# Softmax loop of a one-layer vision tower: class sums and class exponentials taken for two pairs at once

## The chip, the core and the metric

One core of a Trainium2 chip. The metric is the device time of one execution in microseconds, the median of three runs. The profile is of one further execution, with every instruction's start and duration.

## The reference

32 images of 128x128 become 64 patches each. A noisy gated embedding (two linear layers, Mish, product, a third linear layer) gives 64 tokens of 128 features per image, to which the position code is added; a class token is put in front, so an image has 65 tokens. Then one attention layer with 8 heads of 16 features and relative positions in keys and values, and a mixture of 8 experts with the two best per token. What matters here is the attention:

```
attn = softmax((q k^T + q relk[j - i]) / sqrt(128))      # 65 x 65 per image and head
out  = attn v + sum_j attn[i, j] relv[j - i]
h    = h + out Wo + bo
```

All data are float32.

## The kernel before, in words

The program is written engine by engine: each engine has its own list of instructions in a fixed order, and the engines meet only at semaphores. The change lies in the attention's softmax loop. It works on **pairs of images**, 16 of them, numbered p (PAIRS = 16). In the loop the 64 patch queries of two images lie on the 128 partitions after a transpose; the 64 patch keys of 8 heads are 512 columns. The class key's score and the class query's probabilities are kept apart, as 8 columns a pair and one row an image.

Ahead of the loop, eight A2 steps of TensorE make the relative key scores; ScalarE (line 517) and VectorE (line 794) copy each step out of PSUM. From step 4 on TensorE also transposes, after each step, one block of the class key products (turn_cls, line 1224), which VectorE sums (red, line 789).

Iteration p of VectorE's loop, in order (softmax, then the calls behind it), with the short names used below:
- **sum** (line 820): adds the class exponential of pair p-2 to that pair's sum of exponentials; waits for ScalarE.
- **max** (824): over the transposed scores of pair p, in PSUM; waits for TensorE's turn_scores(p) (line 1276).
- **bias** (832): minus the scaled max, or the class score where larger (top and nSc, both in SBUF). ScalarE's exponentials of pair p wait for it.
- **reciprocal** (838) of pair p-2's sum. GpSimd waits for it.
- **class product** (914, odd p from 5): the class key's own share in the output; reads PSUM and vcq.
- **score add** (808): scores of pair p+1 from PSUM plus A2 from SBUF. turn_scores(p+1) waits for it.
- **probability copy** (849, probs(p-3)): the transposed probabilities of pair p-3 from PSUM to PT; waits for TensorE's turn_probs(p-3) (line 1298).
- p = 2: class_scores (859 to 863); p = 3: class_probs (867 to 873), the class query's probabilities p0d and p0x; p = 4: class_turned (883, 884), which puts their transposes into column 64 of PT.
- **value copy** (900) and **class copy** (902), odd p from 7: four images' attended values from PSUM to OT, and their class column to OTc.

ScalarE computes, for each pair, 8 exponentials with row sums (541, one per head) and one of the class column (544). GpSimd, in iteration p: **difference** (374), the class exponent of pair p; **normalisation** (384) of pair p-2's 512 columns by the reciprocal; **class share** (385); in odd iterations **repeat** (392). TensorE, in iteration p: turn_scores(p), scores(p+1), in iteration 4 the transposes of p0d (1344), from p = 15 fillers (keep_warm) and turn_pc, then turn_probs(p-3), which waits for the normalisation of pair p-3 (semaphore pn_ok), then from p = 5 values(p-5); values(0) also waits for class_turned (ptc_ok). The slots of exponentials, SP, are four; bias, sum and reciprocal (ntop, esum, rsum) have two slots.

Behind the loop TensorE runs the relative values, in between with fillers, the output projection and the experts.

## Time and profile before

| | us |
|---|---|
| median of 3 runs | 261.53 (260.9 to 262.17) |
| the profiled execution | 261.36 |
| its span, first to last instruction | 259.5 |
| TensorE busy, matmuls | 236.2 (91%) |
| VectorE busy | 153.7 (59%) |
| ScalarE busy | 132.5 (51%) |
| GpSimd busy | 64.4 (25%) |
| chain of waits, by engine | PE 63%, DVE 17%, issue 6%, ACT 4%, POOL 4%, DMA 4% |

The names in the profile: PE is TensorE's matmul, PEld its weight load, DVE VectorE, ACT ScalarE, POOL GpSimd, SP the engine that issues most transfers. The softmax loop is from about 72 to 118 us of the span. A row's duration includes the end of the engine's pipeline, so a following instruction that waits for nothing starts up to 0.1 us before the row ends; distances from start to start are what add up.

### The profile page before, as it was taken

Reading aid. Unit: us, or ns where it says so; the run is one execution under the profiler, and the core shown is the slowest. Engines: PE = TensorE matmul, PEld = TensorE weight load, DVE = VectorE, ACT = ScalarE, POOL = GpSimd, SP = SyncE. Lnnn points to the kernel's source line nnn. Section 1 sums busy time; section 2 is a strip of 40 time slices with the busy share of each in tenths; the row PEclk is TensorE's granted clock in tenths of the full one; section 3 lists DMA queues with packets and bytes.
Section 4 is the critical chain, followed back from the end, with each engine's and each line's share of the span. In section 5 each row is a group of like instructions: output and inputs, shape, how many; then the busy total and the mean of one; then the engine's idle time right before and its main releaser. Section 6 shows DMA issues by size and latency. Waiting matters only on the chain.

```text
span 259.5 us, 6469 instructions
## 1 busy us (share of the span) xinstructions
PE 236.2 (91%) x2507; PEld 202.2 (78%) x2507; DVE 153.7 (59%) x485; ACT 132.5 (51%) x442; POOL 64.4 (25%) x104
## 2 busy tenths in 40 slices
PE   0989999899886788899999999999999999999994
PEld 0755656599754566677878999799999999999993
DVE  0496798844479999996367749625060605152463
ACT  1543137872179899994047894451708080807100
POOL 8930112087015556667132300000000000000000
PEclk9999999999999999999999999999999999999999
DMA  6970000000003407054000000000000000000015
GB/s 210 287 177 3 0 1 0 0 4 3 3 0 68 98 15 150 4 172 158 5 3 3 0 3 0 4 0 3 1 0 3 0 0 3 0 3 0 1 30 137
DMA packets 10938, 10.05 MB, mean 39 GB/s; under 512 B 1121, under 2 KB 9679, under 8 KB 10780
## 3 DMA queue, kind: packets, MB, share of 16 engines
q1 hardware_dynamic: 8412, 7.88, 11.2%
q10 hardware_dynamic: 1952, 1.41, 1.9%
q8 instruction: 20, 0.33, 0.5%
q0 software_dynamic: 544, 0.35, 0.5%
q14 instruction: 10, 0.08, 0.1%
HBM read 7.52 MB, written 2.11 MB: 37 GB/s over the span
## 4 chain that ended last, share of the span: by engine, by line
PE 63%; DVE 17%; issue 6%; ACT 4%; POOL 4%; DMA 4%; ACTq 1%; DVEq 0%; POOLq 0%
PE banks L1075 58%; DMA region_d<-in_L_tok_W_sw 4%; DVE top L824 4%; DVE stb L808 3%; POOL w_lo L405 2%; ACT region_e L541 2%; PE banks L1276 2%; POOL rstd L338 2%; DVE stb L728 2%; DVE region_c L849 2%; DVE stats L710 1%; DVE h L701 1%; PE banks L1396 1%; ACT w_hi L549 1%; PE banks L1085 1%
## 5 line engine op out<-in xcount | busy, mean ns | idle before, releaser
L1065 DVE SCALAR_TENSOR_TENSOR KT<-banks,vbd,KT 128x128 f32<-128x128 f32 (+1 forms) x136 | 38.0, 342 | 54.3 <-PE banks L1075 53.8
L563 ACT ACTIVATE region_d<-banks,vecs 128x416 f32<-128x416 f32 x80 | 45.5, 610 | 44.5 <-PE banks L1075 44.4
L1075 PE MATMUL banks<-w_all,region_d 128*128 128x128 f32 (+1 forms) x544 | 63.0, 275 | 0.0
L1075 PEld LDWEIGHTS banks<-w_all,region_d 128*128 128x128 f32 (+1 forms) x544 | 61.4, 187 | 1.2 <-ACT region_d L563 0.2
L541 ACT ACTIVATE region_e<-banks,ntop 128x64 f32<-128x64 f32 x128 | 38.7, 362 | 6.5 <-DVE ntop L832 3.5
L541 ACT ACTIVATION_READ_ACCUMULATOR region_e<-banks,ntop 128x1 f32 x128 | 31.8, 255 | 0.0
L1075 PE MATMUL banks<-x_hi,w_hi 128*128 128x416 f32 x80 | 29.9, 373 | 0.0
L1075 PE MATMUL banks<-x_lo,w_hi 128*128 128x416 f32 x80 | 28.2, 353 | 0.0
L1075 PE MATMUL banks<-x_hi,w_lo 128*128 128x416 f32 x80 | 28.2, 352 | 0.0
L1276 PE MATMUL banks<-kc,stb 128*128 128x128 f32 x64 | 10.5, 286 | 8.1 <-DVE stb L808 8.0
L1075 PEld LDWEIGHTS banks<-x_hi,w_hi 128*128 128x128 f32 x80 | 15.1, 188 | 2.4 <-issue 1.2
L384 POOL TENSOR_TENSOR region_e<-region_e,rsum 128x512 f32<-128x512 f32 (+1 forms) x16 | 16.3, 1017 | 0.3 <-PE banks L1323 0.2
L1075 PE MATMUL banks<-kc 128*128 128x128 f32 x56 | 10.3, 314 | 6.5 <-DMA kc<-in_consts 6.5
L1075 PE MATMUL banks<-region_d,relk_bd 64*128 64x64 f32 x256 | 15.3, 288 | 0.0
L1075 PEld LDWEIGHTS banks<-x_lo,w_hi 128*128 128x128 f32 x80 | 15.0, 188 | 0.2
L1075 PEld LDWEIGHTS banks<-x_hi,w_lo 128*128 128x128 f32 x80 | 15.0, 188 | 0.2
L1276 PEld LDWEIGHTS banks<-kc,stb 128*128 128x128 f32 x64 | 6.7, 140 | 10.8 <-DVE stb L808 10.8
L1075 PEld LDWEIGHTS banks<-region_d,relk_bd 64*128 64x128 f32 x256 | 14.6, 188 | 0.6 <-issue 0.5
L1075 PE MATMUL banks<-region_b,wnT 128*128 128x512 f32 x32 | 14.8, 599 | 0.0
L1075 PEld LDWEIGHTS banks<-kc 128*128 128x128 f32 x56 | 8.0, 208 | 7.4 <-DMA kc<-in_consts 6.5
L824 DVE TENSOR_REDUCE top<-banks 128x8 f32<-128x512 f32 x16 | 11.0, 687 | 1.9 <-PE banks L1276 1.4
L1075 PE MATMUL banks<-region_d,region_b 64*128 64x128 f32 x128 | 11.4, 297 | 0.3 <-ACT region_a L517 0.3
(217 smaller groups left out, 367.8 us busy)
## 6 DMA issues: line engine op xcount, KB each, us to landing
region_a<-in_x SPq DMA_DIRECT2D x2, 512.0 KB, 6.3
region_a<-in_x SPq DMA_DIRECT2D x1, 1024.0 KB, 10.7
out<-h SPq DMA_DIRECT2D x2, 512.0 KB, 5.6
h<-out SPq DMA_DIRECT2D x4, 256.0 KB, 4.5
w_sb<-in_L_ffn_W SPq DMA_DIRECT2D x1, 1024.0 KB, 5.6
region_d<-in_L_attn_rel_v SPq DMA_DIRECT2D x2, 260.0 KB, 10.0
out<-KT SPq DMA_DIRECT2D x6, 64.0 KB, 1.8
out<-KT ACTq DMA_DIRECT2D x6, 64.0 KB, 2.0
```

What stands on the lines that cost most here:

```text
L338: g.tensor_tensor(rstd[:, n * TPB:(n + 1) * TPB], ve[:, n * TPB:(n + 1) * TPB], mhalf[:, :], ALU.pow).then_inc(S["rstd_ok"], 1)
L384: g.tensor_tensor(ev, ev, rv, ALU.mult).then_inc(S["pn_ok"], 1)
L405: g.tensor_tensor(w1_lo[:, :], w1_sb[:, :], w1_hi[:, :].bitcast(F32), ALU.subtract).then_inc(S["w1_split"], 1)
L541: last = a.activation(dst[:, h // 2, h % 2], src[:, h // 2, h % 2], ACT.Exp, scale=SCALE, bias=ntop[:, o + h:o + h + 1], accum_out=esum[:, ...
L563: a.activation(HB[:, e % 2, s, blk * FB:(blk + 1) * FB], bank[h_bank(i)][:, 0:FB], ACT.Gelu, bias=vecs[:, v:v + 1]).then_inc(S["gelu_ok"], 1)
L728: last = v.tensor_scalar(ST[n % 2][0:m, i * C:(i + 1) * C], src[0:m, t * C:(t + 1) * C], mv[0:m, 2 * t:2 * t + 1], rstd[0:m, t:t + 1], ALU ...
L808: v.tensor_tensor(ST[p % 2].rearrange("p (g j m) -> p g j m", g=2, j=2), banks[:, 0:1024].rearrange("p (g h j m) -> p g h j m", g=2, h=2, ...
L824: most = mark(v.tensor_reduce(top[:, o].rearrange("p (j s) -> p j s", j=PJ), bank[2 + p % 2][:, :].rearrange("p (j k s) -> p j s k", j=PJ, ...
L849: v.tensor_copy(PT[:, :, 2 * p:2 * p + 2, 0:NPATCH], bank[4 + p % 2][:, :].rearrange("p (j b q) -> p j b q", j=PJ, b=2)).then_inc(S["pt_ok ...
L1065: last = v.scalar_tensor_tensor(acc[0:m, t, :], bank[out_bank(u)][0:m, i * C:(i + 1) * C], comb[0:m, t, e:e + 1], acc[0:m, t, :], op0=ALU. ...
L1075: return t_.matmul(o, l, r, start=start, stop=stop)
L1276: last = t_.transpose(bank[2 + p % 2][:, j * P:(j + 1) * P], ST[p % 2][:, j * P:(j + 1) * P], ident)
```

## The change

- The sums of exponentials, the reciprocals, the differences, the class exponentials and the class shares are computed once for two pairs (in odd iterations; pairs 14 and 15 each by themselves). ntop, esum and rsum get four slots. In VectorE's odd iterations sum and reciprocal stand first, ahead of the max; GpSimd then does the class share of both pairs, the normalisation of pair p-3, the difference, the normalisation of pair p-2.
- The class query's probabilities (p0x, p0d) are made by GpSimd in its iteration 3. Their transposes follow turn_probs(1) in TensorE's iteration 4; class_turned stands in VectorE's iteration 5 and is two copies of one half of the partitions each.
- The value copy takes the class column along (260 columns); OTc becomes a part of OT. A column of zeros in tmpx is set once.
- The A2 steps use other banks; the fourth turn_cls stands behind scores(0), which waits for seven evictions instead of eight.

```diff
+        SPc = region_e[:, :].rearrange("p (n c) -> p n c", n=4)[:, :, 512:520]
+        xnT = sb("xnT", ALL)
         OT = xnT
         OTq = OT[:, :].rearrange("p (q b) -> p q b", b=IMG)
-        OTc = sb("OTc", IMG)
+        OTc = OT[:, TOK:ALL]
...
-        ntop = sb("ntop", 2 * H)
-        esum = sb("esum", 2 * H)
-        rsum = sb("rsum", 2 * H)
+        ntop = sb("ntop", 4 * H)
+        esum = sb("esum", 4 * H)
+        rsum = sb("rsum", 4 * H)
...
-            return (2 if i % 2 == 0 else 0) + g
+            return (2, 4, 0, 2, 0, 2, 0, 2)[i] + g
+
+        def group(p):
+
+            return p // 2 if p < PAIRS - 2 else p - 7
+
+        def closes(p):
+
+            return p % 2 == 1 or p >= PAIRS - 2
+
+        def members(p):
+
+            n = 2 if p < PAIRS - 2 else 1
+            first = (p - n + 1) % 4
+            return n, slice(first, first + n), slice(H * first, H * (first + n))
...
             def difference(p):
 
-                o = slice(8 * (p % 2), 8 * (p % 2) + 8)
+                n, slots, cols = members(p)
                 pool.wait_ge(S["top_ok"], p + 1)
                 if p >= 4:
-                    pool.wait_ge(S["pc_ok"], p - 3)
-                g.tensor_tensor(SP[p % 4][:, 512:520], ntop[:, o], nSc[:, p * H:(p + 1) * H], ALU.subtract)\
+                    pool.wait_ge(S["pc_ok"], group(p - 4) + 1)
+                g.tensor_tensor(SPc[:, slots], ntop[:, cols].rearrange("p (n h) -> p n h", h=H),
+                                nSc[:, (p - n + 1) * H:(p + 1) * H].rearrange("p (n h) -> p n h", h=H), ALU.subtract)\
                     .then_inc(S["dc_ok"], 1)
 
+            def class_share(p):
+
+                n, slots, cols = members(p)
+                pool.wait_ge(S["r_ok"], group(p) + 1)
+                g.tensor_tensor(PcA[:, (p - n + 1) * H:(p + 1) * H].rearrange("p (n h) -> p n h", h=H), SPc[:, slots],
+                                rsum[:, cols].rearrange("p (n h) -> p n h", h=H), ALU.mult).then_inc(S["pc_ok"], 1)
+
             def normalised(p):
 
-                pool.wait_ge(S["r_ok"], p + 1)
-                e_, r_ = SP[p % 4], rsum[:, 8 * (p % 2):8 * (p % 2) + 8]
+                e_, r_ = SP[p % 4], rsum[:, H * (p % 4):H * (p % 4) + H]
                 js = PJ if p < PAIRS - 1 else PJ // 2
                 ev = e_[:, 0:P * js].rearrange("p (j s k) -> p j s k", j=js, s=2)
                 rv = r_[:, 0:2 * js].rearrange("p (j s) -> p j s", j=js).unsqueeze(3).to_broadcast([P, js, 2, NPATCH])
                 g.tensor_tensor(ev, ev, rv, ALU.mult).then_inc(S["pn_ok"], 1)
-                g.tensor_tensor(PcA[:, p * H:(p + 1) * H], e_[:, 512:520], r_, ALU.mult).then_inc(S["pc_ok"], 1)
 
             def repeat(u):
 
-                pool.wait_ge(S["pc_ok"], 2 * u + 2)
+                pool.wait_ge(S["pc_ok"], group(2 * u + 1) + 1)
                 if u >= 2:
                     pool.wait_ge(S["pcT_ps"], u - 1)
                 g.tensor_copy(pc_rep[:, 2 * (u % 2):2 * (u % 2) + 2, :, :].rearrange("p r h d -> p (r h) d"),
                               PcA[:, 16 * u:16 * u + 16].unsqueeze(2).to_broadcast([P, 16, HD]))\
                     .then_inc(S["rep_ok"], 1)
 
+            def class_probs():
+
+                pool.wait_ge(S["cr_ok"], 1)
+                link(g.tensor_tensor(sml[:, 10:12], cv[:, :, NPATCH], sml[:, 8:10], ALU.mult))
+                g.tensor_tensor(p0x[:, :].rearrange("p (r b) -> p r b", b=2),
+                                kc[:, K_PR:K_PR + PAIRS].unsqueeze(2).to_broadcast([P, PAIRS, 2]),
+                                sml[:, 10:12].unsqueeze(1).to_broadcast([P, PAIRS, 2]), ALU.mult)
+                g.tensor_tensor(p0d[:, :].rearrange("p (b s k) -> p b s k", b=2, s=2),
+                                cv[:, :, 0:NPATCH].unsqueeze(2).to_broadcast([P, 2, 2, NPATCH]),
+                                sml[:, 8:10].unsqueeze(2).unsqueeze(3).to_broadcast([P, 2, 2, NPATCH]), ALU.mult)\
+                    .then_inc(S["p0d_ok"], 1)
+
             for p in range(PAIRS + 2):
-                if p < PAIRS:
+                r = p - 2
+                if r >= 0 and closes(r):
+                    class_share(r)
+                    normalised(r - 1 if r < PAIRS - 2 else r)
+                if p < PAIRS and closes(p):
                     difference(p)
-                if p >= 2:
-                    normalised(p - 2)
-                    if p % 2 == 1:
-                        repeat((p - 3) // 2)
+                if 0 <= r < PAIRS - 2 and closes(r):
+                    normalised(r)
+                if p >= 3 and p % 2 == 1:
+                    repeat((p - 3) // 2)
+                if p == 3:
+                    class_probs()
...
                 act.wait_ge(S["top_ok"], p + 1)
                 if p >= 4:
                     act.wait_ge(S["pt_ps"], p - 3)
-                    act.wait_ge(S["pc_ok"], p - 3)
-                if p >= 2:
-                    act.wait_ge(S["r_ok"], p - 1)
-                o = 8 * (p % 2)
+                    act.wait_ge(S["r_ok"], group(p - 4) + 1)
+                o = H * (p % 4)
                 src = bank[2 + p % 2][:, :].rearrange("p (j k s) -> p j s k", j=PJ, s=2)
                 dst = SP[p % 4][:, 0:512].rearrange("p (j s k) -> p j s k", j=PJ, s=2)
                 for h in range(H):
                     last = a.activation(dst[:, h // 2, h % 2], src[:, h // 2, h % 2], ACT.Exp, scale=SCALE,
                                         bias=ntop[:, o + h:o + h + 1], accum_out=esum[:, o + h:o + h + 1])
-                act.wait_ge(S["dc_ok"], p + 1)
-                last = a.activation(SP[p % 4][:, 512:520], SP[p % 4][:, 512:520], ACT.Exp)
                 last.then_inc(S["e_ok"], 1)
+                if closes(p):
+                    n, slots, cols = members(p)
+                    act.wait_ge(S["dc_ok"], group(p) + 1)
+                    a.activation(SPc[:, slots], SPc[:, slots], ACT.Exp).then_inc(S["ec_ok"], 1)
...
-                if r is not None:
-                    q = slice(8 * (r % 2), 8 * (r % 2) + 8)
-                    dve.wait_ge(S["e_ok"], r + 1)
-                    total = mark(v.tensor_tensor(esum[:, q], esum[:, q], SP[r % 4][:, 512:520], ALU.add))
+                if r is not None and closes(r):
+                    n, slots, cols = members(r)
+                    dve.wait_ge(S["ec_ok"], group(r) + 1)
+                    if r >= 4:
+                        dve.wait_ge(S["pn_ok"], r - 3)
+                        dve.wait_ge(S["pc_ok"], group(r - 4) + 1)
+                    total = v.tensor_tensor(esum[:, cols].rearrange("p (n h) -> p n h", h=H),
+                                            esum[:, cols].rearrange("p (n h) -> p n h", h=H), SPc[:, slots], ALU.add)
+                    after(mark(total))
+                    v.reciprocal(rsum[:, cols], esum[:, cols]).then_inc(S["r_ok"], 1)
                 if p is not None:
-                    o = slice(8 * (p % 2), 8 * (p % 2) + 8)
+                    o = slice(H * (p % 2), H * (p % 2) + H)
+                    o4 = slice(H * (p % 4), H * (p % 4) + H)
                     dve.wait_ge(S["s_ps"], p + 1)
                     most = mark(v.tensor_reduce(top[:, o].rearrange("p (j s) -> p j s", j=PJ),
                                                 bank[2 + p % 2][:, :].rearrange("p (j k s) -> p j s k", j=PJ, s=2),
                                                 axis=AX_X, op=ALU.max))
-                if p is not None:
                     after(most)
-                    if p >= 2:
-                        dve.wait_ge(S["e_ok"], p - 1)
-                        dve.wait_ge(S["dc_ok"], p - 1)
-                    v.scalar_tensor_tensor(ntop[:, o], top[:, o], -SCALE, nSc[:, p * H:(p + 1) * H], op0=ALU.mult,
+                    if p >= 4:
+                        dve.wait_ge(S["e_ok"], p - 3)
+                        dve.wait_ge(S["dc_ok"], group(p - 4) + 1)
+                    v.scalar_tensor_tensor(ntop[:, o4], top[:, o], -SCALE, nSc[:, p * H:(p + 1) * H], op0=ALU.mult,
                                            op1=ALU.min).then_inc(S["top_ok"], 1)
-                if r is not None:
-                    after(total)
-                    if r >= 2:
-                        dve.wait_ge(S["pc_ok"], r - 1)
-                    v.reciprocal(rsum[:, q], esum[:, q]).then_inc(S["r_ok"], 1)
...
                 link(v.tensor_reduce(r2, cv, axis=AX_X, op=ALU.add))
-                link(v.reciprocal(sml[:, 8:10], r2))
-                v.tensor_tensor(p0d[:, :].rearrange("p (b s k) -> p b s k", b=2, s=2),
-                                cv[:, :, 0:NPATCH].unsqueeze(2).to_broadcast([P, 2, 2, NPATCH]),
-                                sml[:, 8:10].unsqueeze(2).unsqueeze(3).to_broadcast([P, 2, 2, NPATCH]), ALU.mult)
-                link(v.tensor_tensor(sml[:, 10:12], cv[:, :, NPATCH], sml[:, 8:10], ALU.mult))
-                v.tensor_tensor(p0x[:, :].rearrange("p (r b) -> p r b", b=2),
-                                kc[:, K_PR:K_PR + PAIRS].unsqueeze(2).to_broadcast([P, PAIRS, 2]),
-                                sml[:, 10:12].unsqueeze(1).to_broadcast([P, PAIRS, 2]), ALU.mult)\
-                    .then_inc(S["p0d_ok"], 1)
+                v.reciprocal(sml[:, 8:10], r2).then_inc(S["cr_ok"], 1)
 
             def class_turned():
                 dve.wait_ge(S["p0T_ps"], 1)
-                for b2 in range(2):
-                    pv = bank[6][:, b2 * P:(b2 + 1) * P].rearrange("p (r j s) -> p r j s", r=PAIRS, j=PJ)
-                    tv = ptt[:, :].rearrange("p (r j) -> p r j", j=PJ)
-                    link(v.tensor_scalar(tv, pv[:, :, :, 1], kc[:, K_KP + 1:K_KP + 2], None, ALU.mult))
-                    last = v.scalar_tensor_tensor(PT[:, :, b2:IMG:2, NPATCH].rearrange("p j r -> p r j"),
-                                                  pv[:, :, :, 0], kc[:, K_KP:K_KP + 1], tv, op0=ALU.mult,
-                                                  op1=ALU.add)
-                    if b2 == 0:
-                        link(last)
+                for s in range(2):
+                    hs = slice(NPATCH * s, NPATCH * (s + 1))
+                    last = v.tensor_copy(PT[hs, :, :, NPATCH].rearrange("p j (r b) -> p j r b", b=2),
+                                         bank[6][hs, 0:256].rearrange("p (b r j s) -> p j r b s", b=2, r=PAIRS, j=PJ)
+                                         [:, :, :, :, s])
                 last.then_inc(S["ptc_ok"], 1)
...
-                v.scalar_tensor_tensor(OTq[:, :, 4 * u:4 * u + 4].rearrange("p q b -> p b q"), o[:, :, 0:NPATCH],
-                                       vecs[:, V_BV:V_BV + 1], own(u), op0=ALU.add, op1=ALU.add)
-                v.tensor_copy(OTc[:, 4 * u:4 * u + 4], o[:, :, NPATCH]).then_inc(S["w1_ev"], 1)
+                v.scalar_tensor_tensor(OT[:, :].rearrange("p (q b) -> p q b", b=IMG)[:, :, 4 * u:4 * u + 4]
+                                       .rearrange("p q b -> p b q"), o,
+                                       vecs[:, V_BV:V_BV + 1], own(u), op0=ALU.add, op1=ALU.add).then_inc(S["w1_ev"], 1)
...
-                if p == 4:
+                if p == 5:
...
-                if i >= 4:
+                if 4 <= i < 7:
                     turn_cls(i - 4)
 
             def scores(p):
                 if p == 0:
-                    pe.wait_ge(S["a2_evA"], 8)
-                    pe.wait_ge(S["a2_evD"], 8)
+                    pe.wait_ge(S["a2_evA"], 7)
+                    pe.wait_ge(S["a2_evD"], 7)
...
+            turn_cls(3)
             for p in range(PAIRS + 5):
                 if p < PAIRS:
                     turn_scores(p)
...
-                if p == 4:
-                    pe.wait_ge(S["p0d_ok"], 1)
-                    for b2 in range(2):
-                        last = t_.transpose(bank[6][:, b2 * P:(b2 + 1) * P], p0d[:, b2 * P:(b2 + 1) * P], ident)
-                    last.then_inc(S["p0T_ps"], 1)
...
                     turn_probs(p - 3)
+                if p == 4:
+                    pe.wait_ge(S["p0d_ok"], 1)
+                    for b2 in range(2):
+                        last = t_.transpose(bank[6][:, b2 * P:(b2 + 1) * P], p0d[:, b2 * P:(b2 + 1) * P], ident)
+                    last.then_inc(S["p0T_ps"], 1)
                 if p >= 5:
                     values(p - 5)
```

## Rows read from the trace of the kernel before

**Rows 1.** Windows view, one steady period: length, then busy us and count by engine.

```profile
94.11:99.53 5.42, 4.72 (x70) 3.48 (x68) 5.28 (x17) 5.07 (x37) 3.13 (x7) 1.00 0.53 115
```

**Rows 2.** Timeline, VectorE, one period: start us, duration us, engine, line, operation.

```profile
94.18 0.68 DVE L824 TENSOR_REDUCE top<-banks 128x8 f32<-128x512 f32 x1
94.89 0.17 DVE L832 SCALAR_TENSOR_TENSOR ntop<-top,nSc 128x8 f32<-128x8 f32 x1
...
95.09 0.67 DVE L808 TENSOR_TENSOR stb<-banks,region_a 128x512 f32<-128x512 f32 x1
95.68 0.68 DVE L849 COPY region_c<-banks 128x512 f32<-128x512 f32 x1
96.28 0.15 DVE L820 TENSOR_TENSOR esum<-esum,region_e 128x8 f32<-128x8 f32 x1
96.51 0.69 DVE L824 TENSOR_REDUCE top<-banks 128x8 f32<-128x512 f32 x1
...
97.44 0.42 DVE L914 TENSOR_TENSOR tmpx<-banks,vcq 128x256 f32<-128x256 f32 x1
97.79 0.68 DVE L808 TENSOR_TENSOR stb<-banks,region_a 128x512 f32<-128x512 f32 x1
...
98.98 0.65 DVE L900 SCALAR_TENSOR_TENSOR xnT<-banks,vecs,tmpx 128x256 f32<-128x256 f32 x1
99.48 0.16 DVE L902 COPY OTc<-banks 128x4 f32<-128x4 f32 x1
```

**Rows 3.** Timeline, GpSimd and TensorE in the same period.

```profile
95.14 0.20 POOL L374 TENSOR_TENSOR region_e<-ntop,nSc 128x8 f32<-128x8 f32 x1 [1.23 <-DVE ntop L832]
95.30 1.04 POOL L384 TENSOR_TENSOR region_e<-region_e,rsum 128x512 f32<-128x512 f32 x1
...
95.82 0.66 PE L1276 MATMUL banks<-kc,stb 128*128 128x128 f32 x4 [0.47 <-DVE stb L808]
```

**Rows 4.** Timeline, VectorE: a sum and its reciprocal with nothing between.

```profile
115.20 0.15 DVE L820 TENSOR_TENSOR esum<-esum,region_e 128x8 f32<-128x8 f32 x1
115.39 0.20 DVE L838 RECIPROCAL rsum<-esum 128x8 f32<-128x8 f32 x1
```

**Rows 5.** Timeline: VectorE instructions beside GpSimd ones, at two places.

```profile
77.67 1.05 POOL L384 TENSOR_TENSOR region_e<-region_e,rsum 128x512 f32<-128x512 f32 x1
...
78.39 0.34 DVE L861 TENSOR_SCALAR sml<-sml 128x2 f32<-128x2 f32 x1
...
88.31 0.40 POOL L392 COPY region_d<-PcA 128x256 f32<-128x256 f32 x1
...
88.53 0.20 DVE L820 TENSOR_TENSOR esum<-esum,region_e 128x8 f32<-128x8 f32 x1
```

**Rows 6.** Timeline, VectorE: from the last A2 eviction to the first probability copy.

```profile
68.92 0.69 DVE L794 COPY region_a<-banks 128x512 f32<-128x512 f32 x1 [1.27 <-PE banks L1075]
...
70.47 0.69 DVE L808 TENSOR_TENSOR stb<-banks,region_a 128x512 f32<-128x512 f32 x1 [0.85 <-PE banks L1075]
...
79.10 0.16 DVE L820 TENSOR_TENSOR esum<-esum,region_e 128x8 f32<-128x8 f32 x1
...
80.65 0.68 DVE L849 COPY region_c<-banks 128x512 f32<-128x512 f32 x1
```

**Rows 7.** Timeline: class scores, first values, max of pair 6, half normalisation.

```profile
78.77 0.29 DVE L862 TENSOR_TENSOR cx<-banks,sml 128x128 f32<-128x128 f32 x1
...
86.22 0.44 PE L1075 MATMUL banks<-region_c,vbd 128*32 128x65 f32 x16
...
88.77 0.69 DVE L824 TENSOR_REDUCE top<-banks 128x8 f32<-128x512 f32 x1
...
117.15 0.61 POOL L384 TENSOR_TENSOR region_e<-region_e,rsum 128x256 f32<-128x256 f32 x1 [0.25 <-PE banks L1323]
```

**Rows 8.** Timeline, TensorE: transposed probabilities of pairs 12 and 13.

```profile
112.83 0.60 PE L1298 MATMUL banks<-kc,region_e 128*128 128x128 f32 x4
...
115.03 0.66 PE L1298 MATMUL banks<-kc,region_e 128*128 128x128 f32 x4
```

More of the change, by code:

```diff
@@ L913, in class_key @@
                     dve.wait_ge(S["w1_ev"], u - 1)
-                v.tensor_tensor(own(u), bank[u % 2][:, 256:512].rearrange("p (b q) -> p b q", q=NPATCH),
+                v.tensor_tensor(own(u)[:, :, 0:NPATCH], bank[u % 2][:, 256:512].rearrange("p (b q) -> p b q", q=NPATCH),
                                 vcq[:, :].unsqueeze(1).to_broadcast([P, 4, NPATCH]), ALU.mult)\
@@ L949, in attended_class @@
                 dve.wait_ge(S["w2_ps"], 5)
-                link(v.scalar_tensor_tensor(OTc[:, :], bank[4][:, 0:IMG], vecs[:, V_BV:V_BV + 1], OTc[:, :],
-                                            op0=ALU.add, op1=ALU.add))
-                v.scalar_tensor_tensor(OTc[:, :], bank[4][:, IMG:2 * IMG], clsv[:, 5:6], OTc[:, :], op0=ALU.mult,
+                link(v.tensor_tensor(OTc, bank[4][:, 0:IMG], OTc, ALU.add))
+                v.scalar_tensor_tensor(OTc, bank[4][:, IMG:2 * IMG], clsv[:, 5:6], OTc, op0=ALU.mult,
                                        op1=ALU.add).then_inc(S["oc_ok"], 1)
@@ L1441, in _ @@
             pe.wait_ge(S["oc_ok"], 1)
-            mm(bank[6][0:IMG, 0:C], OTc[:, :], wo).then_inc(S["opc_ps"], 1)
+            mm(bank[6][0:IMG, 0:C], OTc, wo).then_inc(S["opc_ps"], 1)
             pe.wait_ge(S["w1_split"], 1)
```

17 lines of the change are left out of this document (8 added, 9 removed).

## The prediction

> **What bounds the kernel now.** I read the page first: its engine table and slices say that TensorE is busy nearly everywhere and always at the full granted clock (1.0, the 2.4 GHz level), except in the slices of the softmax loop, 72 to 118 us, where VectorE shows nines and TensorE fives to nines. The chain of waits says the same: inside the loop it runs over VectorE's instructions, with a short hop to TensorE for each transpose. Behind the loop it is TensorE again, without a gap worth naming, so a shift of the loop's end moves the end of the kernel by the same amount. Then the windows: in one steady period of two pairs VectorE is busy 5.28 of 5.42 us, ScalarE 5.07, TensorE 4.72, GpSimd 3.13 [rows 1]. VectorE's own issue order is the bound; ScalarE is close behind. The loop is a fixed order of waits, so I read one period instruction by instruction [rows 2] and worked out the same period, and then the start and the tail, with the new order.
>
> I count from an odd iteration's class sum. Start to start on VectorE [rows 2]: max to bias 0.71; bias over reciprocal to score add 0.20 (I split it 0.09 and 0.11); score add to probability copy 0.59; probability copy to whatever follows 0.60; class product to score add 0.35; value copy to class copy 0.50 and 0.05 from there to the next sum, at 99.53, the window's edge [rows 1]; sum to max 0.07. A max cannot start before its transposes are done: 0.69 from their start at 95.82 to 96.51 [rows 2, 3].
>
> **The period, part by part.** *Removed from VectorE:* in even iterations the sum (0.07) and the reciprocal (0.11); the class copy (0.05), for which the value copy grows from 256 to 260 columns (+0.01, estimated from its 0.50). In odd iterations sum and reciprocal stay, but the reciprocal now stands before the max and waits for the sum: 0.19 [rows 4], then 0.11 to the max. Before, the max waited for TensorE anyway (sum at 96.28, max at 96.51), so the max moves from 0.23 to 0.30. The bias follows at 1.01, the class product at 1.10, the score add at 1.45 and the probability copy could start at 2.04. Had nothing else to be waited for, the period would be 2.04 + 0.60 + 0.51 + 0.71 + 0.09 + 0.59 + 0.60 = 5.14, or 0.29 less than now.
>
> *ScalarE:* half of the class exponentials go, and its wait for the reciprocal becomes one for the bias alone. It is 0.35 short of the period already [rows 1], so this is worth nothing while VectorE sets the pace, and it would be needed only below about 5 us.
>
> *The new wait, GpSimd to TensorE to VectorE.* The reciprocal of pairs p-3 and p-2 now comes in iteration p, and the same iteration copies out the transposed probabilities of pair p-3. Before, pair p-3 was normalised one iteration earlier. So in each odd iteration: reciprocal at 0.19, its 0.20 and 0.08 to GpSimd (bias at 94.89 with 0.17, GpSimd at 95.14) [rows 2, 3] gives 0.47; the class share in front costs 0.16 to the next instruction [rows 3] and I take 0.18 for its 16 columns; the normalisation runs from 0.65 to 1.69 (1.04 [rows 3]); TensorE starts 0.06 later (the score add ends at 95.76, transposes 95.82) at 1.75; the copy can start at 2.44. That is 0.40 after the 2.04. By itself this makes the period 5.54, already 0.11 longer than now. Behind the waiting copy on VectorE stand the value copy and the even max; on TensorE the values and the next transposes stand behind the waiting transposes, but end before VectorE wants them (1.75 + 1.0 + 0.69 = 3.44 against 3.70).
>
> *Two engines on one port.* Now the normalisation (0.65 to 1.69) lies across the odd bias (1.01), which reads two SBUF tensors, top and nSc. Today it never does: the normalisation always starts after the bias. What happens when they meet is seen at two places [rows 5]. The scalar operation on two columns at 78.39 takes 0.34 and ends at 78.73, and the normalisation beside it ends at 78.72. The sum at 88.53 takes 0.20 where rows 2 and 4 have 0.15, and ends at 88.73, with the GpSimd copy beside it ending at 88.71. Instructions that read PSUM and one SBUF tensor, the score add and the probability copy from 95.09 on, run through a normalisation unchanged (0.67, 0.68) [rows 2, 3]. So I let the bias end at 1.69 + 0.02 = 1.71 instead of 1.18; the class product then starts at 1.65 (0.08 before that end, as all followers do), the score add at 2.00, the probability copy at 2.59, which is later than its 2.44, the value copy at 3.19, even max 3.70, bias 4.41, score add 4.50, probability copy 5.09, next sum 5.69. **Period 5.69, +0.26.** The bound below for this hold is 0 (then 5.54); the bound above is the normalisation's whole 1.04 on the bias (+0.4 more), and I take the value by the row at 78.39.
>
> The Trainium skill (SBUF — State Buffer, section "Who interferes with whom") states this as a rule: a VectorE instruction with two SBUF inputs contends with a GpSimd instruction that reads SBUF, and whoever comes first holds the shared ports for its whole instruction. The two rows agree with it.
>
> **Start of the loop.** Scores of pair 0 no longer stand behind the fourth class transpose nor behind the last eviction. They are over by about 69.6, and the score add starts when the last eviction ends, 68.92 + 0.69 = 69.61, so at 69.65 instead of 70.47 [rows 6]: -0.82. The bank change in the eight A2 steps: TensorE had no gap there, so 0. Iteration 2 loses a reciprocal (-0.11). The sum of iteration 3 moves from 79.10 [rows 6] to 78.17. But iteration 3 is the first odd one: its probability copy comes at 78.17 + 2.44 = 80.61, against 80.65 now [rows 6]. The 0.93 us are gone.
>
> **Class query.** In iteration 3 a reduction and a reciprocal remain (0.6 + 0.42 with the copy before them, estimated from instructions of their size), so max 4 starts at 81.63. GpSimd gets its operands at 81.80, does two small ones (0.27 and 0.20, as in rows 3 with one wait) and the 256 columns in 0.61 (the half normalisation of rows 7), until 82.88. Bias 4 wants to start at 82.34 and reads two SBUF tensors: held to 82.90. Score add 82.84, copy 83.43, sum 5 at 84.03. Iteration 5 has the period's waits: copy at 86.62. Then the class column, two copies of 128 columns at 0.29 [rows 7], 87.22 to 87.83. Moved here, they now gate the values of pair 0, which stand before the next score transposes in TensorE's order: 87.89, 0.40 for the 16 matmuls (the row at 86.22 has 0.44 with the pipeline's end), 0.69 for the transposes: **max 6 at 88.98, against 88.77 [rows 7]: +0.21.** All of the shorter class code is spent in this wait. The bounds: 0.9 earlier, if the values did not stand in the way, or 0.3 later, if the 64-row copies take as long as they would for twice the columns.
>
> **To the end of the loop.** Sum 7 comes 0.71 + 0.09 + 0.59 + 0.60 = 1.99 later, at 90.97, sum 9 at 96.66 (now 96.28), +0.38; three more periods at +0.26 give sum 15 at 113.74, +1.16. In iteration 15 no score add is left to fill VectorE, and the last ones behind it are set by TensorE: transposes of pair 12 now start at 112.83 [rows 8], then at 113.74 + 1.75 = 115.49: +2.66. Values, ten filler matmuls and the transposes of pair 13 follow 2.20 later as now (115.03 [rows 8]); in today's kernel those fillers covered a wait, now they lie on the path. One class copy less on VectorE gives back 0.06. **Sum: -0.82 - 0.11 + 1.14 (to max 6) + 0.17 + 0.78 + 1.50 - 0.06 = +2.60.** The profiled execution took 261.36 us for a span of 259.5, against the median of 261.53; 261.36 + 2.60 = 263.96 and 261.53 + 2.60 = 264.13, so I say 264.0.
>
> **Rivals.** *A, both waits as argued: 264.0, chance 0.45,* its own range 263.2 to 265.2. *B, the bias is not held:* only the GpSimd to TensorE wait remains. Iteration 4 gives 0.39 back, iteration 5 0.15, the four later periods 0.60: +1.46, 262.8. For it: the held rows are a scalar operation and a sum, none is a bias. 0.17. *C, faster:* normalisation ends before VectorE needs the copy, so the released instructions count in full: -0.93 at the start, six periods at -0.29 (-1.74), class parts about -1.0 (five small instructions less): 257.7. It decides from where the way from sum to copy takes less than 2.04 instead of 2.44; against it, every link of the 2.44 is a row. With ScalarE bounding, or half of the waits, it is 259 to 260. 0.12. *D, no change:* the waits are each some 0.2 shorter and the tail's 1.5 is partly absorbed, which leaves 260.5 to 262.5. For it: GpSimd spans are rough. 0.16. *E, more contention:* the class product, whose vcq is in SBUF, and the copies are held too, 0.2 a period and more in the tail: 265.8. 0.10.
>
> **Numbers.** A change under 0.5% (1.3 us) cannot be told from none here. Range 261.0 to 266.0: it leaves out most of C and the lower edge of D. Slower is A, E and half of B, with a little of D: 0.66; same is the rest of B and D: 0.23; faster 0.11.
>
> **What would show it.** Right: in odd iterations of the profile after, the bias takes some 0.6 to 0.7 us instead of 0.17 and ends with the normalisation; the period is 5.7; max 6 is preceded by a wait for TensorE behind values 0; in the tail the transposes of pair 12 wait for GpSimd and start 2.7 later. Wrong, if the period is under 5.43, or the bias keeps its 0.17 (B), or the probability copies of odd iterations follow the score add at once (C).

## The result, and the profile after

| | before | after |
|---|---|---|
| median, us | 261.55 (260.90 to 262.17, 4 runs) | 266.05 (265.40 to 268.82, 4 runs) |
| profiled execution, us | 261.36 | 266.37 |
| its span, us | 259.5 | 264.6 |
| mean granted clock of TensorE | 1.0 | 0.993 (the other three runs: 0.979, 0.992, 0.992) |

The ratio is 1.0192 (95%: 1.0116 to 1.0269): slower by 4.5 us, where 2.6 was predicted. The median lies 0.05 us above the predicted range. Ratios, here and below, leave out executions that took over 1.5% longer than the fastest of the same kernel.

The page of the kernel after: engine totals, then the slices of TensorE, VectorE, GpSimd and TensorE's granted clock.

```profile
PE 238.9 (90%) x2507; PEld 205.1 (78%) x2507; DVE 154.9 (59%) x459; ACT 132.1 (50%) x435; POOL 63.2 (24%) x93
...
PE   0999999899976698779999999999999999999993
...
DVE  0485798844579789998176838636060515152553
...
POOL 8930112187006345557312300000000000000000
PEclk9999999999999899999999999999999999999999
```

TensorE is busy 2.7 us longer with the same 2507 matmuls, and one slice of its clock is an 8, where the page of before has nines throughout. The steady periods and the stretch in front of them, by windows (columns as in [rows 1]; the clock is the third from the end):

```profile
104.61:110.32 5.71, 4.73 (x68) 3.48 (x67) 5.61 (x14) 5.05 (x35) 2.79 (x5) 1.00 0.02 3
...
90.00:92.00 2.00, 2.00 (x15) 1.48 (x13) 1.55 (x3) 0.77 (x5) 0.00 (x0) 0.61 0.03 8
92.00:94.00 2.00, 2.00 (x24) 1.55 (x22) 1.08 (x4) 1.70 (x12) 0.55 (x2) 0.54 0.02 8
```

The period is 5.71 us against 5.42 [rows 1]. TensorE and ScalarE do in it what they did before; VectorE has three instructions fewer (14 against 17), and yet is busy 0.33 longer. Its timeline shows why (start, duration):

```profile
104.61 0.17 DVE L862 TENSOR_TENSOR esum<-esum,region_e 128x16 f32<-128x16 f32 x1
104.81 0.25 DVE L865 RECIPROCAL rsum<-esum 128x16 f32<-128x16 f32 x1
104.97 0.63 DVE L870 TENSOR_REDUCE top<-banks 128x8 f32<-128x512 f32 x1
105.64 0.74 DVE L877 SCALAR_TENSOR_TENSOR ntop<-top,nSc 128x8 f32<-128x8 f32 x1
106.31 0.41 DVE L942 TENSOR_TENSOR tmpx<-banks,vcq 128x256 f32<-128x256 f32 x1
106.64 0.67 DVE L847 TENSOR_TENSOR stb<-banks,region_a 128x512 f32<-128x512 f32 x1
107.24 0.68 DVE L889 COPY region_c<-banks 128x512 f32<-128x512 f32 x1
```

and GpSimd's and TensorE's beside it (in brackets the idle time before a row, and what ended it):

```profile
105.14 0.22 POOL L397 TENSOR_TENSOR PcA<-region_e,rsum 128x16 f32<-128x16 f32 x1 [2.83 <-DVE rsum L865]
105.32 1.04 POOL L406 TENSOR_TENSOR region_e<-region_e,rsum 128x512 f32<-128x512 f32 x1
```

```profile
106.42 0.66 PE L1325 MATMUL banks<-kc,region_e 128*128 128x128 f32 x4 [0.75 <-POOL region_e L406]
```

The odd bias takes 0.74 instead of 0.17 and ends at 106.38; the normalisation beside it ends at 106.36. TensorE's transposes wait 0.75 for the same normalisation. Both predicted waits stand in these ten rows.

Ahead of the periods, TensorE in iterations 5 and 6:

```profile
89.24 0.44 PE L1102 MATMUL banks<-region_c,vbd 128*32 128x65 f32 x16 [1.68 <-DVE region_c L913]
89.61 0.66 PE L1303 MATMUL banks<-kc,stb 128*128 128x128 f32 x4
90.20 1.03 PE L1102 MATMUL banks<-region_d,region_b 64*128 64x128 f32 x8
91.16 1.11 PE L1325 MATMUL banks<-kc,region_e 128*128 128x128 f32 x4
```

The values of pair 0 have waited 1.68 us for class_turned. Right behind it four transposes take 1.11 instead of 0.66, while the windows show the granted clock at 0.61 and 0.54: for 3.4 us the clock was on the 1.2 GHz level (0.5 of the full one). The kernel before idles too, 1.42 us in its longest wait here, and keeps its clock:

```profile
88.07 0.66 PE L1276 MATMUL banks<-kc,stb 128*128 128x128 f32 x4 [1.42 <-DVE stb L808]
```

The waits of the kernel after in 72 to 124 us (total, times, longest):

```profile
PE banks L1325 <- POOL region_e L406: 5.7, 6, 1.4
DVE top L870 <- PE banks L1303: 3.3, 4, 1.2
```

The milestones, each as a difference of start times on VectorE or TensorE, put the whole beside the forecast. "Clock held" is a kernel of the experiments (fill_all).

| stretch | before | forecast | after | clock held |
|---|---|---|---|---|
| last A2 eviction to max 6 | 19.85 | +0.21 | +0.52 | +0.53 |
| max 6 to sum 9 | 7.51 | +0.17 | +1.08 | +0.22 |
| sum 9 to sum 15 (three periods) | 16.30 | +0.78 | +0.84 | +0.83 |
| sum 15 to the first relative value | 7.55 | +1.44 | +1.29 | +1.31 |
| sum | 51.21 | +2.60 | +3.73 | +2.89 |

The span grew by 5.1: 3.73 here, 0.36 behind the loop, and 1.01 before it. The eight A2 steps, whose banks are changed, have no part in the 1.01: from the first of their evictions on VectorE to the last it is 14.81 before and 14.82 after. In front of them the change alters no instruction. The last eviction started anywhere from 68.4 to 70.0 in the profiles of all kernels, and at 69.93, 69.28 and 68.73 in the three of the changed one, so the 1.01 is scatter of one profile.

### The profile page after: what moved, and what is told of

It is laid out like the page before. It is cut to its first block, busy times and chain, and to the rows that moved or that the text cites. A ratio compares the mean times of both kernels' runs of the same rounds, so it can differ in the third digit from the quotient of the medians.

```text
span 264.6 us, 6397 instructions
## 1 busy us (share of the span) xinstructions
PE 238.9 (90%) x2507; PEld 205.1 (78%) x2507; DVE 154.9 (59%) x459; ACT 132.1 (50%) x435; POOL 63.2 (24%) x93
## 4 chain that ended last, share of the span: by engine, by line
PE 63%; DVE 18%; issue 7%; POOL 4%; ACT 3%; DMA 3%; SPq 1%; DVEq 0%; POOLq 0%
PE banks L1102 58%; DVE top L870 3%; DVE region_c L889 3%; DMA rows<-in_L_tok_W_sb 3%; DVE stb L847 2%; POOL w_lo L444 2%; POOL rstd L353 2%; DVE stb L767 2%; PE banks L1112 1%; DVE stats L749 1%; PE banks L1303 1%; ACT region_e L578 1%; DVE h L740 1%; PE banks L1424 1%; ACT w_hi L588 1%
## 5 line engine op out<-in xcount | busy, mean ns | idle before, releaser
L578 ACT ACTIVATION_READ_ACCUMULATOR region_e<-banks,ntop 128x1 f32 x128 | 28.7, 226 | 0.0
L1102 PE MATMUL banks<-kc 128*128 128x128 f32 x56 | 11.4, 341 | 6.5 <-DMA kc<-in_consts 6.5
L1325 PE MATMUL banks<-kc,region_e 128*128 128x128 f32 x64 | 10.8, 293 | 5.8 <-POOL region_e L406 5.7
L1102 PEld LDWEIGHTS banks<-kc 128*128 128x128 f32 x56 | 9.1, 234 | 7.4 <-DMA kc<-in_consts 6.5
L1325 PEld LDWEIGHTS banks<-kc,region_e 128*128 128x128 f32 x64 | 7.1, 145 | 8.1 <-POOL region_e L406 6.9
```

The source lines that it names most:

```text
L578: last = a.activation(dst[:, h // 2, h % 2], src[:, h // 2, h % 2], ACT.Exp, scale=SCALE, bias=ntop[:, o + h:o + h + 1], accum_out=esum[:, ...
L1102: return t_.matmul(o, l, r, start=start, stop=stop)
L1325: last = t_.transpose(bank[4 + p % 2][:, j * P:(j + 1) * P], SP[p % 4][:, j * P:(j + 1) * P], ident)
```

## Experiments

All experiments run beside the kernel before, whose medians were 262.02, 262.02, 261.35 and 261.61 in the four groups. My theory was the prediction's: two waits, the clock a third cause that it had left out. The rivals: the class query's order, contention elsewhere, or the clock as the whole loss.

**1. One half of the change at a time.** pair_only is the kernel before with sums, reciprocals, differences and class exponentials of two pairs. rest_early is the opposite: no pairing, everything else of the change, with class_turned in iteration 4.

```
rest_early: sum, reciprocal, difference, normalisation, class share per pair, as before
            GpSimd makes p0x, p0d; class column in the value copy; scores(0) early
-                if p == 5:      # class_turned
+                if p == 4:
```

> The kernel before with the pairing alone: sums, reciprocals, differences, class exponentials and class shares for two pairs. No other start of the loop, class query on VectorE as before, class column copied by itself. Theory of the two waits (late normalisation, bias held beside it): period of two pairs 5.71 plus 0.05 for the class copy against 5.43, in the tail the transposes of pair 12 another 1.5 later: together +3.0 to +4.0, 264.5 to 265.5. Rival (the pairing is harmless, the class parts and the clock make the loss): 261 to 262.

> The changed kernel without the pairing (sums, reciprocals and exponentials pair by pair as before), with the early start of the loop, GpSimd's class probabilities and the class column in the value copy, and class_turned in iteration 4. Theory: no late normalisation and no held bias, so the gains count: 0.7 at the start, 0.5 to 0.7 for the class query, 0.05 a period for the class copy: 259.5 to 260.3. Rival (the other edits gain nothing because another engine sets the pace): 261.5.

Measured: pair_only 266.59, over its forecast of 264.5 to 265.5, ratio 1.0176 (1.0149 to 1.0203), period 5.77; its clock fell once, behind a wait of 1.95 us in front of the transposes. rest_early 259.14, under its forecast of 259.5 to 260.3, ratio 0.9893 (0.9874 to 0.9911): faster than both kernels by more than the interval. Its period:

```profile
92.01:97.38 5.37, 4.72 (x72) 3.48 (x70) 5.22 (x15) 5.05 (x37) 3.13 (x7) 1.00 0.52 111
```

The pairing alone costs 4.6 us, as much as the whole change; the rest alone gains 2.9. From the last A2 eviction to the first relative value pair_only takes 4.95 longer than before and rest_early 1.86 less; the other 1 us of rest_early's gain in the times stands in no stretch of the loop.

rest_late is rest_early with class_turned back in iteration 5, as the change has it:

```
-                if p == 4:
+                if p == 5:
```

> As e6_rest_early, but with class_turned in iteration 5, as the change has it. Theory: the first values wait behind it on TensorE and max 6 comes 0.5 to 1.2 us later than with class_turned in iteration 4: 259.7 to 260.3 beside 259.1, and the clock may fall once. Rival: nothing, 259.1.

Measured: 261.21 (10 runs), ratio 0.9983 (0.9946 to 1.0019), no change. Max 6 comes 0.94 later behind the last eviction than in rest_early, and TensorE shows why:

```profile
88.17 0.44 PE L1091 MATMUL banks<-region_c,vbd 128*32 128x65 f32 x16 [1.97 <-DVE region_c L902]
```

So moving class_turned costs about 1 us on the path. In the times it costs more, and the forecast of 259.7 to 260.3 missed: rest_late is 0.4 under the kernel before beside it, rest_early 2.9. Part of this goes with the clock: rest_late's five executions at a mean clock of 0.997 or more took 260.7 on average, the five at 0.993 or less 262.0. In this profile the clock held in spite of 1.97 us of idle time: the idle place makes the fall possible, not certain.

The two halves as the change has them, +4.6 and −0.4, come near its 4.5. What rest_early gains is not kept beside the pairing: rest_early has its first probability copy 0.71 sooner behind the last eviction than the kernel before, the changed kernel 0.06 later, because there the copy waits for the normalisation.

**2. The class query's wait in the changed kernel.** early_turn sets class_turned back to iteration 4; fill keeps it in 5 and gives TensorE six filler matmuls in front of the values of pair 0.

```
early_turn:
-                if p == 5:      # VectorE, class_turned
+                if p == 4:
fill:
+                if p == 5:
+                    keep_warm(6, spare=7)
```

> The changed kernel with class_turned in VectorE's iteration 4 instead of 5; its input is there (transposes end at 84.46, VectorE arrives at 85.11). Theory: TensorE's wait of 1.7 us for the class column goes and with it the fall of the clock; max 6 comes about 1.2 us earlier and the stretch behind it 0.9 shorter, so about 263.9. Rival: the two copies (0.77 us) delay sum 5, normalisation and all behind it by as much as they save, 265.5 or more.

> The changed kernel with six filler matmuls on TensorE ahead of the first values, where TensorE stands idle for 1.7 us behind the class column (89.24). The wait itself stays. Theory K (the clock): the granted clock does not fall to 0.5 behind this idle time, so the stretch from max 6 to sum 9 shrinks from 8.59 us to about 7.7, and the kernel gains 0.9 us, about 265.1. Rival W (only the waits count, the clock costs nothing on the path): nothing, 266.0. If the fillers outlast the wait, up to 0.2 is lost.

Measured: early_turn 265.46, ratio 1.0135 (1.0116 to 1.0154); fill 266.03, ratio 1.0152 (1.0134 to 1.0171). In early_turn the wait for class_turned is gone and max 6 comes 0.91 sooner behind the last eviction, but the clock fell all the same, in the transposes behind the wait for the normalisation:

```profile
87.52 0.66 PE L1325 MATMUL banks<-kc,region_e 128*128 128x128 f32 x4 [1.57 <-POOL region_e L406]
...
90.06 1.11 PE L1325 MATMUL banks<-kc,region_e 128*128 128x128 f32 x4
```

In fill the clock held where the fillers were (max 6 to max 8 took 5.75, against 6.60 after; the forecast had 5.69), but fell earlier, in an idle place that they did not cover:

```profile
80.00:82.00 2.00, 0.92 (x6) 0.72 (x7) 1.68 (x4) 1.73 (x13) 1.90 (x4) 0.86 0.00 0
82.00:84.00 2.00, 2.00 (x13) 1.44 (x12) 1.93 (x5) 1.66 (x12) 1.51 (x5) 0.50 0.39 89
```

Neither forecast held in the time: there is more than one place for the fall. fill's 266.03 is what the rival (the clock costs nothing) had. Its two executions at a mean clock of 0.998 and 1.0 took 265.96 and 266.11, the two at 0.994 and 0.992 took 266.82 and 265.61: in these times no gain of a held clock can be seen.

**3. The pairing's two waits, one at a time.** recip_behind puts the double reciprocal behind the bias, so that the bias cannot be held and the normalisation comes later. share_behind lets GpSimd do the first normalisation before the class share.

```
share_behind:
+                    pool.wait_ge(S["r_ok"], group(r) + 1)
-                    class_share(r)
                     normalised(r - 1 if r < PAIRS - 2 else r)
+                    class_share(r)
```

> The changed kernel with the reciprocal of two pairs behind the bias again, as in the kernel before. The normalisation of GpSimd then starts after the bias. Theory of the held port: the odd bias is back at 0.17 us (0.74 in the changed kernel), although nothing about the bias itself changed; but the normalisation starts 0.84 later, so the probability copy waits longer for it and the period grows from 5.71 to about 6.4: 270. Rival (the bias takes 0.74 because its operands have four slots now): it stays at 0.74.

> The changed kernel with GpSimd's class share behind the first normalisation instead of ahead of it. Theory: the normalisation starts and ends 0.18 earlier in each odd iteration, and the held bias and all behind it with it: period 5.53 instead of 5.71, seven odd iterations, 1.2 us in all: 264.8. Rival (VectorE's own order sets the period): nothing, 266.0.

Measured: recip_behind has the ratio 1.044 (1.0379 to 1.0502) and the period 6.44, where 6.4 was forecast. Its time missed the forecast of 270: the profiled execution took 272.50 us, with a mean clock of 0.978, the other three 274.48 to 282.51. VectorE:

```profile
101.35 0.17 DVE L876 SCALAR_TENSOR_TENSOR ntop<-top,nSc 128x8 f32<-128x8 f32 x1
...
103.73 0.69 DVE L891 COPY region_c<-banks 128x512 f32<-128x512 f32 x1 [1.18 <-PE banks L1327]
```

The bias has its 0.17 again, and the other wait takes its place in full. share_behind: 264.81, ratio 1.012 (1.008 to 1.0161), forecast 264.8:

```profile
103.71 1.04 POOL L406 TENSOR_TENSOR region_e<-region_e,rsum 128x512 f32<-128x512 f32 x1 [2.80 <-DVE rsum L866]
```

```profile
104.21 0.57 DVE L878 SCALAR_TENSOR_TENSOR ntop<-top,nSc 128x8 f32<-128x8 f32 x1
```

The normalisation starts 0.18 sooner behind its sum (0.53 instead of 0.71), the held bias ends 0.17 sooner (1.60 behind the sum instead of 1.77), and the period is 5.54 instead of 5.71. Both waits hang on when the first normalisation ends.

two_mends has early_turn and share_behind together.

> Both mends on the changed kernel: class_turned in iteration 4 and the class share behind the first normalisation. If the effects add: 266.0 less 2.1 less 1.2 is 262.7, still over the kernel before, because the tail and the late normalisation stay. Rival: they overlap, 263.5 or more.

Measured: 263.54, ratio 1.0056 (1.002 to 1.0091), 0.8 above the forecast and on the rival's 263.5: the two gains overlap. From the last eviction to the first relative value it takes 1.19 more than the kernel before, again with a fall of the clock, at 80.8 to 84 us.

**4. Is it the port?** Two kernels are the kernel before with GpSimd work laid beside the odd bias: one reads SBUF and writes it (a product of 640 columns), the other only writes it (two memsets of 544 columns).

```
read_beside:
+    pool.wait_ge(S["s_ps"], p + 1)          # odd p from 5
+    g.tensor_tensor(w1_lo[:, 0:640], kc[:, 0:640], kc[:, 0:640], ALU.mult)
write_beside, behind the same wait:
+    [link(g.memset(rt[:, :], 0.0)) for _ in range(2)]
```

> The kernel before with one added instruction on GpSimd in odd iterations from 5: a product of 640 columns that reads SBUF twice, started with the max, so that it runs beside the odd bias. Its result is not used. Theory of the held port: the odd bias ends with it, 0.17 us grows to 0.5 to 0.8 us. Rival (the bias was long in the changed kernel for its own form or operands): it stays at 0.17.

> The kernel before with two added fills of 544 columns on GpSimd, started with the max in odd iterations from 5, which write SBUF and read nothing. Theory (what is held is the reading side): the odd bias keeps 0.17 us. Rival (any GpSimd instruction beside it holds the bias): 0.3 us or more. The first normalisations may start a little later, the period grows by no more than 0.2.

Measured, one execution each: 263.53 and 261.91. Reading, GpSimd and VectorE:

```profile
97.28 1.25 POOL L399 TENSOR_TENSOR w_lo<-kc 128x640 fp32r<-128x640 f32 x1
```

```profile
97.96 0.59 DVE L835 SCALAR_TENSOR_TENSOR ntop<-top,nSc 128x8 f32<-128x8 f32 x1
```

Writing:

```profile
96.87 1.16 POOL L399 MEMSET rt<- 128x544 f32 x2
```

```profile
97.57 0.17 DVE L835 SCALAR_TENSOR_TENSOR ntop<-top,nSc 128x8 f32<-128x8 f32 x1
```

A GpSimd operation that reads SBUF holds the bias until it ends (97.96 + 0.59 = 98.55, against 97.28 + 1.25 = 98.53); one that only writes leaves it at 0.17. The Trainium skill (SBUF — State Buffer, section "Who interferes with whom") says the same of a VectorE instruction with two SBUF inputs, and the trace agrees, with 0.59 and 0.17. Of the two rows from which the prediction priced the hold, only the sum at 88.53 has two SBUF tensors; the operation at 78.39 reads one, and a scalar for each partition. A bias with one input in PSUM was not tried.

**5. What the clock costs.** no_tail_fill takes out the fillers of iterations 16 and 17. fill_both lays fillers over three waits of TensorE in iterations 3 and 5; fill_all adds four in front of the transposes of pair 12. The two controls are the changed kernel itself, timed in the same groups.

```
no_tail_fill:
-                    keep_warm(5 if p == PAIRS else 3, spare=0)
fill_both:
+                if p == 3:
+                    pe.wait_ge(S["cx_ok"], 1)
+                if p in (3, 5):
+                    keep_warm(4 if p == 3 else 2, spare=7)    # before turn_probs(p - 3)
+                if p == 5:
+                    keep_warm(5, spare=7)                     # before values(0)
fill_all, also:
+                if p == PAIRS - 1:
+                    pe.wait_ge(S["pcx_ok"], 5)
+                    keep_warm(4, spare=0)
```

> The changed kernel without the sixteen filler matmuls of iterations 16 and 17. Theory: in the changed tail they lie on the path (1.31 and 0.77 us between transposed probabilities and values), so the relative values start about 1 us earlier if the clock holds: 265.0. Rival: the clock falls behind the now idle TensorE, the following matmuls take twice their time for some us, and the kernel is slower than the changed one, 267.

> The changed kernel with fillers on TensorE at all three idle places of the loop's start: four ahead of the first transposed probabilities, two ahead of those of pair 2, five ahead of the first values. With the fillers of one place alone the clock had fallen at the other place (80.3 to 84). Theory K: the granted clock stays at 1.0 through the loop, the stretch from the last A2 eviction to max 8 takes about 26.1 us (26.97 in the changed kernel, whose clock falls at 90) and the kernel gains 0.9: about 265.1 where the changed one has 266.0. Rival: the clock falls all the same, or the fillers outlast the waits: no gain.

> The changed kernel itself once more, on the chip and in the rounds of e10_fill_both, as its measure: 266 with the clock falling once for 3 to 4 us between 80 and 94.

> The changed kernel with fillers at every idle place, those of e10_fill_both and four more ahead of the transposed probabilities of pair 12, where the clock fell in e10_fill_both (117 to 121). Theory K: no fall is left, the mean clock of its runs is 0.998 or more, and the kernel is 0.9 us (one fall at the start) to 2.4 us (both) faster than the changed kernel beside it: about 264.7 where that has 266 to 267. What is left over the kernel before, some 3 us, is then the waits alone. Rival: no difference beyond the interval; the falls lie where VectorE sets the pace.

> The changed kernel once more as the measure of e14_fill_all: 266 to 268, mean clock 0.978 to 0.993.

Measured:

| kernel | median | ratio (95%) |
|---|---|---|
| no_tail_fill | 267.52 | 1.0213 (1.018 to 1.0247) |
| fill_both | 266.18 | 1.0164 (1.0095 to 1.0233) |
| changed kernel beside it | 267.77 | 1.0228 (1.0171 to 1.0285) |
| fill_all | 265.38 | 1.0174 (1.0121 to 1.0227) |
| changed kernel beside it | 266.99 | 1.0218 (1.0153 to 1.0284) |

Without its tail fillers the kernel loses the clock a second time, as the rival had it (267; the theory had 265.0). TensorE waits 1.39 us for pair 12, as in the kernel after, then idles in short pieces, and from the third row on it is slow (0.66 where the same matmuls took 0.44). TensorE and the windows:

```profile
118.14 0.66 PE L1325 MATMUL banks<-kc,region_e 128*128 128x128 f32 x4 [1.39 <-POOL region_e L406]
118.72 0.44 PE L1102 MATMUL banks<-region_c,vbd 128*32 128x65 f32 x16
...
120.05 0.66 PE L1102 MATMUL banks<-region_c,vbd 128*32 128x65 f32 x16
```

```profile
120.00:122.00 2.00, 1.62 (x22) 1.00 (x21) 1.92 (x7) 1.98 (x7) 1.21 (x3) 0.52 1.09 324
122.00:124.00 2.00, 2.00 (x23) 1.49 (x22) 1.69 (x4) 1.92 (x2) 1.36 (x3) 0.50 0.99 271
124.00:126.00 2.00, 2.00 (x37) 1.17 (x39) 1.11 (x3) 0.00 (x0) 1.99 (x1) 0.50 0.07 15
```

The fillers did lie on the path: while the clock still held, the transposes of pair 13 started 1.35 behind those of pair 12, against 2.17 with fillers. The fall took more than that back.

In fill_both the clock held at the start and fell in the tail instead:

```profile
116.00:118.00 2.00, 1.57 (x22) 1.24 (x23) 1.61 (x4) 1.68 (x13) 1.90 (x4) 0.77 0.90 300
118.00:120.00 2.00, 2.00 (x11) 2.00 (x11) 0.59 (x3) 1.98 (x9) 1.23 (x3) 0.50 1.09 345
```

In fill_all it held through the loop. A window of its start, where the kernel after had 0.61, and the same two of the tail:

```profile
90.00:92.00 2.00, 2.00 (x32) 1.44 (x28) 1.93 (x6) 1.38 (x10) 0.00 (x0) 1.00 0.00 0
...
116.00:118.00 2.00, 1.64 (x26) 1.38 (x27) 1.61 (x4) 1.68 (x12) 1.85 (x4) 1.00 1.02 348
118.00:120.00 2.00, 2.00 (x32) 1.74 (x31) 1.34 (x6) 1.98 (x8) 1.20 (x2) 1.00 1.07 329
```

From sum 15 to the first relative value fill_all takes 8.86 and fill_both 10.45: a fall in the tail costs 1.6. At the start the kernel after lost 0.86 (the table's 1.08 against 0.22). The control of the first group had both falls, the one at the start 6.8 us long, and took 57.72 from eviction to relative values: 6.5 over the kernel before and 3.6 over fill_all, 2.06 of it at the start.

The times say less than the stretches. Both forecasts, 265.1 and 264.7, were missed. Each pair of fillers and control differs by 1.6 us in the median, but the intervals overlap, and one execution of fill_all had a mean clock of 0.991 and took 268.05. The other three, at 0.997 to 0.999, took 265.10 to 265.43, hardly less than the better two of the changed kernel beside them (265.11 and 265.86, at 0.991 and 0.990). A further fall is plain: of the changed kernel's twelve executions in all groups, the six at a mean clock of 0.987 to 0.993 took 265.9 on average and the six at 0.978 or 0.979 took 268.2. All twelve stand at 0.993 or less, and so do only 5 of the 33 executions of the kernel before from which the four groups' ratios are taken: it is the change that makes the falls common. What the first fall costs in the whole time is not known closer than 0 to 1.6 us; on the path of the profiled execution it is 0.86.

## Why the prediction was right in direction and short in size

- **Period (5.69, +0.26): right.** 5.72, 5.71, 5.71. The held bias was forecast to end with the normalisation, 1.71 behind the sum; it ends at 1.77. The normalisation starts at 0.71 instead of 0.65, because the reciprocal of 16 columns takes 0.25 where [rows 4] had that of 8 with 0.20. recip_behind shows the port wait and the wait for the transposes to be separate, share_behind that one early end shortens both, read_beside and write_beside that reading SBUF is what holds the bias. Rival B falls: the bias is held.
- **Start (−0.82, lost by iteration 3): right.** The score add starts 0.82 behind the last eviction, against 1.55 [rows 6]: 0.73 sooner. The first probability copy, forecast level with before, is 0.06 later.
- **Class query (+0.21): right in kind, +0.52 in size.** Max 6 stands behind the wait for class_turned as forecast. Bias 4 is held as forecast (0.56 long) and copy 5 is 0.10 late. The short term was the class copies: from copy 5 to the values of pair 0 I had 1.27, from the durations in [rows 7], and it is 1.51, with 0.77 for the two copies instead of 0.61.
- **Tail (+1.44): +1.29.** The transposes of pair 12 start 5.0 later than [rows 8] and 1.80 behind sum 15, forecast 1.75; the filler matmuls lie on the path, as argued and as no_tail_fill shows.
- **The step that failed: "always at the full granted clock".** I took the clock of before as given, from one profiled execution, and no term and no rival asked what it would do. The change leaves TensorE idle for 1.35 us in iteration 3, 1.68 in iteration 5 and 1.39 in iteration 15, and the clock falls behind one or two of these places. (The kernel before, with 1.42 as its longest wait there, loses the clock in some executions too.) With the clock held, the loop measures +2.89 against the forecast 2.60. In the profiled execution the fall adds 0.86 at the start; in others it comes in the tail too. This is the term "+0.17 to sum 9", which measured +1.08, and +0.22 with the clock held.
- **The rest.** The median is 2.05 above the 264.0. The fall accounts for 0.86, the other terms of the loop for 0.3, and 0.4 to 0.5 lies at the very end, where I had forecast no change. It is not TensorE's: from the first relative value to the start of VectorE's last group of instructions it is 133.78 before and 133.67 after. From there to the end, where the last output transfers run, it is 5.59 before and 6.06 after, and so it is in every profile: 5.58 to 5.65 in the kernel before, with or without added GpSimd work, and in the kernels with one half of the change, 5.98 to 6.35 in all with both halves. The cause of this stays open; nothing was tried on it. What is left, some 0.5, is within what the front of the program scatters by, and is not explained either. That the median ended only 0.05 outside the range says nothing for the mechanism: the clock had no place in the range. The group of VectorE that is meant, before and after:

```profile
253.91 2.40 DVE L1065 SCALAR_TENSOR_TENSOR KT<-banks,vbd,KT 128x128 f32<-128x128 f32 x8 [0.66 <-PE banks L1075]
258.54 2.40 DVE L1092 SCALAR_TENSOR_TENSOR KT<-banks,vbd,KT 128x128 f32<-128x128 f32 x8 [0.66 <-PE banks L1102]
```

- Rival C (faster) had its core right in one respect: some of the edits do pay, 2.9 us in rest_early, but they are those that do not pair. Rival E's number, 265.8, is close to the result by another cause: the class product (0.41) and the copies (0.68) are not held.

## What to carry to other kernels

Taking small work for two rounds at once saves its fixed costs and delays the first round's consumers by a round; count the new distance from producer to consumer before the savings, which here were 0.07 and 0.11 us a period against a wait that the prediction worked out at 0.40. Check for each VectorE instruction with two SBUF inputs, however small, whether the new order lays a GpSimd instruction that reads SBUF across it. And where a change opens an idle place on TensorE, give the clock a term of its own: here 0.9 to 2.1 us on the path for a fall, possible but not certain. In the profiled executions only fillers at all four of the long waits held it, and not in every other execution.

## What the runs showed of the hardware that was not expected

- The fall of the clock moves: filled at 88 us, it came at 81; filled there too, at 117; filled there too, not at all in the profiled execution. Each lasted 3.4 us, but 6.8 in the tail without fillers and at the start of one control.
- An instruction of 8 columns is held for as long as GpSimd's runs: 0.17 became 0.74, 0.59 or 0.57, until 0.02 or 0.03 behind the end of GpSimd's instruction.
- An idle time of 1.97 us left the clock at 1.0 in one kernel, while it fell behind 1.57 in early_turn and 1.17 in two_mends. How long TensorE idles at one place does not by itself tell whether the clock falls.
